# A graph transformer layer on one core: first normalisation tile by tile, query units by channel block, and a new order in the last two groups

## The reference

```python
nx = layernorm(x, ln1_g, ln1_b)
q, k, v = nx @ Wq + bq, nx @ Wk + bk, nx @ Wv + bv        # 8 heads of 64
scores = where(adj, q @ k.T / sqrt(64), -1e9)             # per graph and head
x = x + (softmax(scores) @ v) @ Wo + bo
nx = layernorm(x, ln2_g, ln2_b)
return x + gelu(nx @ W1 + b1) @ W2 + b2                   # 512 -> 2048 -> 512
```

## Time and profile before

| | |
|---|---|
| median of 3 runs | 2164.35 us (2162.98 to 2164.65) |
| profiled execution | 2164.58 us, span 2162.7 us |
| TensorE busy | 2127.7 us, 98% of the span |
| VectorE busy | 1487.9 us, 69% |
| ScalarE busy | 905.2 us, 42% |
| POOL busy | 433.7 us, 20% |
| chain that ended last | PE 96%, DVE 1%, ACT 1%, POOL 1%, DMA 1% |

### The profile page before, as it was taken

How to read it: one execution, slowest core, us unless ns; L and a number is a source line. 1 busy time by engine, 2 the same in 40 slices (tenths; PEclk the granted TensorE clock), 3 DMA queues, 4 the chain that set the end, 5 groups by cost and what they waited for, 6 DMA issues and landing times.

```text
span 2162.7 us, 33121 instructions
## 1 busy us (share of the span) xinstructions
PE 2127.7 (98%) x13216; PEld 1756.9 (81%) x13216; DVE 1487.9 (69%) x2205; ACT 905.2 (42%) x1318; POOL 433.7 (20%) x291
## 2 busy tenths in 40 slices
PE   7999999999999988999999999999999999999999
PEld 6788888888888876888888888888888888888887
DVE  4888888888999965666666656656666666656433
ACT  3444444443344443345345345345345345345332
POOL 2333433321111114003003003003003103103200
PEclk9999999999999998999999999999999999999999
DMA  4344333331222114444544544544544544544532
GB/s 147 129 153 156 135 133 133 138 124 65 70 75 70 46 50 185 156 180 172 193 180 165 199 180 165 199 174 171 199 167 173 204 160 174 209 153 174 217 126 93
DMA packets 103793, 323.98 MB, mean 150 GB/s; under 512 B 21360, under 2 KB 29552, under 8 KB 87280
## 3 DMA queue, kind: packets, MB, share of 16 engines
q1 hardware_dynamic: 98144, 321.68, 40.4%
q10 hardware_dynamic: 5520, 0.55, 0.2%
HBM read 265.57 MB, written 56.62 MB: 149 GB/s over the span
## 4 chain that ended last, share of the span: by engine, by line
PE 96%; DVE 1%; ACT 1%; POOL 1%; DMA 1%; issue 0%; SPq 0%; ACTq 0%; DVEq 0%; POOLq 0%
PE lin L181 11%; PE lin L182 10%; PE lin L183 10%; PE ps_r L181 5%; PE ps_r L182 5%; PE ps_r L183 5%; PE ps_out L181 5%; PE ps_out L182 5%; PE ps_out L183 5%; PE ps_x L181 5%; PE ps_x L182 5%; PE ps_x L183 5%; PE ps_z L181 3%; PE ps_z L182 3%; PE ps_z L183 3%; PE ps_scores L1334 2%
## 5 line engine op out<-in xcount | busy, mean ns | idle before, releaser
L1168 DVE TENSOR_TENSOR acc<-ps_r,acc 128x512 f32<-128x512 f32 x256 | 176.5, 690 | 327.8 <-PE ps_r L183 327.0
L798 ACT ACTIVATE snaps<-ps_x 128x512 f32<-128x512 f32 x192 | 114.4, 596 | 410.7 <-PE ps_x L183 410.7
L181 PE MATMUL ps_r<-w_ring,h_ring 128*128 128x512 f32 x512 | 199.6, 390 | 0.9 <-DVE h_ring L1158 0.9
L181 PE MATMUL ps_x<-nxc,w_ring 128*128 128x512 f32 x512 | 199.4, 389 | 0.0
L183 PE MATMUL ps_r<-w_ring,h_ring 128*128 128x512 f32 x512 | 199.2, 389 | 0.0
L183 PE MATMUL ps_x<-nxc,w_ring 128*128 128x512 f32 x512 | 199.2, 389 | 0.0
L182 PE MATMUL ps_x<-nxc,w_ring 128*128 128x512 f32 x512 | 199.2, 389 | 0.0
L182 PE MATMUL ps_r<-w_ring,h_ring 128*128 128x512 f32 x512 | 199.2, 389 | 0.0
L181 PE MATMUL ps_out<-w_ring,h_ring 128*128 128x512 f32 x512 | 199.2, 389 | 0.0
L183 PE MATMUL ps_out<-w_ring,h_ring 128*128 128x512 f32 x512 | 199.2, 389 | 0.0
L182 PE MATMUL ps_out<-w_ring,h_ring 128*128 128x512 f32 x512 | 199.2, 389 | 0.0
(11 more groups left out here) (131 smaller groups left out, 5131.1 us busy)
## 6 DMA issues: line engine op xcount, KB each, us to landing
w_ring<-w_scratch SPq DMA_DIRECT2D x64, 1792.0 KB, 7.3
w_ring<-w_scratch SPq DMA_DIRECT2D x64, 1024.0 KB, 7.1
xb<-x_scratch SPq DMA_DIRECT2D x22, 1024.0 KB, 10.2
xres<-in_x SPq DMA_DIRECT2D x64, 256.0 KB, 2.8
x_scratch<-xres SPq DMA_DIRECT2D x64, 256.0 KB, 2.2
x<-in_x SPq DMA_DIRECT2D x15, 1024.0 KB, 6.0
acc<-x_scratch SPq DMA_DIRECT2D x32, 256.0 KB, 2.9
out<-xb SPq DMA_DIRECT2D x32, 256.0 KB, 2.0
```

What stands on the lines that cost most here:

```text
L181: pe.matmul(out, lhs[1], rhs[0], start=first, stop=False, skip_group_check=resumed)
L798: act.activation(snaps[:, j], ps_x[:, :], ACT.Copy).then_inc(snap_done[j], 1)
L1168: dve.tensor_tensor(acc(t), ps_r[:, :], acc(t), ALU.add).then_inc(acc_added, 1)
```

## The change

**Start.** The statistics, the aggregation, the addition of epsilon, POOL's power and the norm of group 0 are done tile by tile (`first_stats`), and `var_done` and `rstd_done` count four for group 0. The transposes of group 0 go to the banks of scores and probabilities (`first_t`) instead of `lin`. `wq` comes in four transfers and is split in four pieces: ScalarE does three before the first `affine` and the fourth behind the first `nx_hi`, VectorE all four low parts. The query units are done together (`first_queries`): for each channel block c, all four units. The transposes of group 1 stand before the last three value units of group 0, and ScalarE does the four `affine` of group 1 first and then the four `nx_hi`. The statistics of group 1 come after the splits of group 0 as before.

**Last two groups.** SP issues the loads of `spare` first in every group body that has them. ScalarE does `ln_tile_affine` of tile 6 before its second `take_probT` of group 14 and that of tile 7 behind it. POOL's four sums move from group 14, where they stood before the last two biases, to group 15, behind its first `fill_neg`. In TensorE's order for group 15 F5 and P1 stand before W0.

```diff
-              ("W", 0), ("F", 5), ("P", 1), ("W", 1), ("O", 1), ("F", 6), ...
+              ("F", 5), ("P", 1), ("W", 0), ("W", 1), ("O", 1), ("F", 6), ...
...
-        return [("U", j) for j in FIRST_UNITS if g == -1] + [("T", k) for k in range(KC)]
+        units = [("U", j) for j in FIRST_UNITS]
+        return units[:-3] + [("T", k) for k in range(KC)] + units[-3:] if g == -1 else []
...
             def body(g, par):                       # SP
+                for n in ln_tiles(g):
+                    load_ln_tile(n)
                 if g + 3 < NG:
                     load_x(g + 3, 1 - par)
...
-                for n in ln_tiles(g):
-                    load_ln_tile(n)
...
-            for i, w in enumerate((wq, wk, wv)):
+            for c in range(KC):
+                sp.dma_start(raw_w[0][:, c], wq[c * P:(c + 1) * P, :]).then_inc(wq_loaded[c], 16)
+            for i, w in ((1, wk), (2, wv)):
...
-                if g == NG - 2:                     # POOL, body
-                    t_sums(0)
-                    for n in range(4):
-                        t_sum(0, n)
                 bias_xres(g, 2)
                 bias_xres(g, 3)
             def last_body(g):
                 fill_neg(g, 0)
+                t_sums(0)
+                for n in range(4):
+                    t_sum(0, n)
                 conv_lo(0)
...
-            rstd_of(0)
-            weight_lo(0, slice(KC // 2, KC))
+            for t in range(TILES):
+                pool.wait_ge(var_done, t + 1)
+                pool.tensor_tensor(rstd[:, t:t + 1], var_eps[:, t:t + 1], minus_half[:, 0:1], ALU.pow)\
+                    .then_inc(rstd_done, 1)
...
+                for n in ln_tiles(g)[:-1]:          # ACT, body
+                    ln_tile_affine(n)
                 take_probT(g, 1)
+                if g == NG - 2:
+                    ln_tile_affine(ln_tiles(g)[-1])
                 unit(9)
...
-            weight_hi(0)
+            wq_hi(0)
+            wq_hi(1)
+            wq_hi(2)
             act.wait_ge(cols_loaded, 16 * 4)
             for k in range(KC):
                 affine(0, k)
                 nx_hi(0, k)
+                if k == 0:
+                    wq_hi(3)
...
+            def first_stats(t):                     # DVE
+                ln_stats(0, 0, t)
+                dve.wait_ge(stats_done, t + 1)
+                dve.bn_aggr(moments[:, t, :], stats[:, t, :]).then_inc(moments_done, 1)
+                dve.wait_ge(moments_done, t + 1)
+                dve.tensor_scalar(var_eps[:, t:t + 1], moments[:, t, 1:2], EPS, None, ALU.add).then_inc(var_done, 1)
...
+            for t in range(TILES):
+                first_stats(t)
+                if t > 0:
+                    ln_norm(0, 0, t - 1)
+            ln_norm(0, 0, TILES - 1)
+            for c in range(3):
+                wq_lo(c)
+            for k in range(KC):
+                nx_lo(0, k)
+                if k == 0:
+                    wq_lo(3)
...
+            def first_queries():                    # PE
+                for c in range(KC):
+                    pe.wait_ge(w_lo_done[0], c + 1)
+                    pe.wait_ge(nx_split, c + 1)
+                    for m in range(KC):
+                        mm = split3(pe, lin[bank_of(-1, "U", 3 * m)][:, :],
+                                    tuple(w[0][:, c, m * P:(m + 1) * P] for w in (w_hi, w_lo)),
+                                    (nxT_hi[:, c, :], nxT_lo[:, c, :]), c == 0, c == KC - 1)
+                        if c == KC - 1:
+                            mm.then_inc(u_done, 1)
```

More of the change, by code:

```diff
@@ L298, in adj_layer @@
             ps_part = {"C11": ps_y, "C22": ps_z, "C12": ps_z}
+        first_t = [ps[:, i * HEADS // 2:(i + 1) * HEADS // 2] for ps in (ps_scores.rearrange("p h t n -> p h (t n)"), ps_probT)
+                   for i in range(2)]
+        first_t = [b.rearrange("p h n -> p (h n)") for b in first_t]
         raw_w = [qT[1][:, :, :], v[1][:, :, :], softmax.rearrange("p s (h m) t n -> p (s h) (m t n)", h=2), qT[1][:, :, :]]
@@ L310, in adj_layer @@
         w_loaded, w_hi_done, w_lo_done = ([sem(f"w{c}_{s}") for c in "qkvo"] for s in ("loaded", "hi_done", "lo_done"))
+        wq_loaded = [sem(f"wq_loaded{c}") for c in range(KC)]
         cols_loaded, rows_loaded, mlp_cols_loaded = sem("cols_loaded"), sem("rows_loaded"), sem("mlp_cols_loaded")
@@ L505, in _ @@
             load_mask(0, 0)
-            sp.wait_ge(w_lo_done[0], 2)
+            sp.wait_ge(w_lo_done[0], KC)
             sp.dma_start(raw_w[3], wo.rearrange("(c p) n -> p c n", p=P)).then_inc(w_loaded[3], 16)
@@ L531, in rstd_of @@
             def rstd_of(g):
-                pool.wait_ge(var_done, g + 1)
+                pool.wait_ge(var_done, TILES + g)
                 pool.tensor_tensor(rstd[:, :], var_eps[:, :], minus_half[:, :], ALU.pow).then_inc(rstd_done, 1)
@@ L754, in body @@
                         nx_hi(g + 2, k)
-                for n in ln_tiles(g):
-                    ln_tile_affine(n)
+                if g < NG - 2:
+                    for n in ln_tiles(g):
+                        ln_tile_affine(n)
             def job_hi(q, which):
@@ L864, in mlp_step, with wq_hi @@
                         m_affine(2 * s + (q == 6), k)
-            weight_hi(0)
+            def wq_hi(c):
+                act.wait_ge(wq_loaded[c], 16)
+                act.activation(w_hi[0][:, c, :], raw_w[0][:, c], ACT.Copy).then_inc(w_hi_done[0], 1)
+            wq_hi(0)
+            wq_hi(1)
+            wq_hi(2)
             act.wait_ge(cols_loaded, 16 * 4)
@@ L1247, in mlp_step, with wq_lo @@
                     conv_lo(s + 1, 3)
-            for g in range(2):
-                for t in range(TILES):
-                    ln_stats(g, g, t)
-                ln_var(g)
-                for t in range(TILES):
-                    ln_norm(g, g, t)
-                if g == 0:
-                    weight_lo(0, slice(0, KC // 2))
-                    for k in range(KC):
-                        nx_lo(0, k)
-                    weight_lo(2, slice(0, KC))
+            def wq_lo(c):
+                dve.wait_ge(w_hi_done[0], c + 1)
+                dve.tensor_tensor(w_lo[0][:, c, :], raw_w[0][:, c], w_hi[0][:, c, :].bitcast(F32),
+                                  ALU.subtract).then_inc(w_lo_done[0], 1)
+            for t in range(TILES):
[5 more added lines that the diff above has]
+                wq_lo(c)
+            for k in range(KC):
+                nx_lo(0, k)
+                if k == 0:
+                    wq_lo(3)
+            weight_lo(2, slice(0, KC))
+            for t in range(TILES):
+                ln_stats(1, 1, t)
+            ln_var(1)
+            for t in range(TILES):
+                ln_norm(1, 1, t)
             weight_lo(3, slice(0, KC))
@@ L1305, in unit @@
                 if is_first(g) and m == 0:
-                    pe.wait_ge(w_lo_done[which], 2 if which == 0 else 1)
+                    pe.wait_ge(w_lo_done[which], 1)
                 for c in range(KC):
@@ L1385, in body @@
                     elif kind == "U":
-                        unit(g + 1, n, take_bank(g, "U", n))
+                        if is_first(g + 1) and n % 3 == 0:
+                            if n == 0:
+                                first_queries()
+                        else:
+                            unit(g + 1, n, take_bank(g, "U", n))
                     elif kind == "O":
```

10 lines of the change are left out of this document (5 added, 5 removed).

## The result

The changed kernel takes 2148.5 us (median of 6 runs, 2148.22 to 2150.96), the kernel before in the same comparison 2163.35 us (median of 6, 2161.71 to 2164.65). The ratio is 0.9934 with a 95% interval of 0.9922 to 0.9947: faster, by 14.3 us by the ratio and 14.9 by the medians. The forecast was 13.0 us and 2151.4 us. The profiled execution took 2148.46 us with a span of 2146.4, so the two profiles lie 16.3 us apart in span, since the one of before stood above its median.

What follows compares the result with a forecast made beforehand. TensorE's own work bounds the steady groups; idle time lies before 60 us and from 770 to 842 us. 3.3 + 1.3 + 5.4 + 3.0 = 13.0 us off 2164.35 gives 2151.4 us, range 2146.5 to 2157.5.

Steps and rivals of the forecast that it cites:

- Part 1: Start, group 0 tile by tile: first product 3.3 us earlier, moved transposes of group 1 1.3 us more; 4.6 us.
- Part 2: Group 14, spare loads first: prob wait goes, but a new 2.9 us attT_lo wait before W0; 0.3 to 1.9 us left.
- Part 3: Group 15, POOL's sums after biases and memset: O0 5.4 us earlier, after a new wait of about 4.0 us.
- Part 4: Group 15, F5 and P1 before W0: 4.5 us loss at W0 goes, new slow stretch at O0 costs 1.7; 3.0 us.
- No meetings: Rival, groups 14 and 15: POOL and VectorE pass each other, norm 6 is not held; 2147.8 us, 20%.
- Pieces land together: Rival, start and end: wq pieces land at once, and more POOL and VectorE meetings; 2155 to 2156.4 us, 16%.
- the end gives nothing: Rival, last groups: stores, tile and xres loads collide, only the start is left; 2159.8 us or within 0.2%, 6%.
- The slower case: Rival, group 15: POOL's sums 1 and 2 hold conv_hi and the softmax, some 20 us late; 2168.7 us, 3%.

Runs made afterwards that it cites:

- experiment 10: Changed kernel with wq loaded in one transfer, all four pieces waiting for it: 2149.22 us, ratio 0.9937.
- Experiment 3: Kernel before with only SP's tile loads moved first in its group bodies: 2162.75 us, ratio 0.9997.
- experiment 1: Changed kernel with its last two groups as before, so only the start is new: 2158.92 us, ratio 0.9979.
- experiment 8: Changed kernel with POOL's low splits in group 15 held back until prob of unit 0 is done: 2153.57 us, ratio 0.9958.
- Experiment 5: Changed kernel with POOL's a_rstd of tile 6 ahead of the two biases of group 14: 2147.4 us, repeated 2146.87 us.
- experiment 4: Changed kernel with W0 back in front of F5 and P1 in group 15: 2152.87 us, ratio 0.995.
- experiment 2: Kernel before with only the edits of groups 14 and 15, start as before: 2152.72 us, ratio 0.9951.
- experiment 6: Changed kernel with a_rstd of tile 6 before group 14's biases and group 15's second memset before the low splits: 2145.8 us, repeated 2147.07 us.
- experiment 7: Changed kernel with only the second memset of group 15 moved ahead of the first low split: 2151.55 us, ratio 0.9949.

## Why the prediction was right, and where its sizes were off

**Part 1, the start: right.** The first product was forecast 3.3 us earlier and came 3.2 us earlier. Between it and the first scores of group 0 another 1.1 us came that was not in the sum: the low level lasted 3.5 us where I had taken the 5.7 of before. It is near the lower of the two bounds that I gave (3.2 to 8 us; no profile shows 8). This 1.1 us is luck of the profiled execution as much as a gain: nine profiles have the changed kernel's start; in eight of them the low level of these products lasted from 2.7 to 5.7 us, in the ninth there was none. In the nine the first scores of group 0 start between 48.28 and 50.95, in the three profiles with the start of before between 53.73 and 54.47. The moved transposes gave 1.05 us instead of 1.3, since the second query unit of group 1 still waits 0.8 us for its low half. From 4.6 forecast to 5.1 in the profile, and 4.5 to 4.8 us when timed alone. The pieces from one queue landed one after another (experiment 10). The Trainium skill (DMA: Bandwidth & Descriptors, section Two DMAs through the same engine are not ordered) warns that a later transfer may complete before an earlier one; no run here shows that.

**Part 2, loads first: right in the mechanism, the wait too small.** The wait for `prob` went, and a wait for `attT_lo` took its place, because `a_rstd` stood behind two biases and a memset. I had 2.9 us with a slow stretch as possible, and it was 3.84 us with a slow stretch (granted 0.57, some 1.6 us). The step that was off is the moment of the biases. In before's clock the norm came at 774.8 (769.71 + 5.1) and not at 773.4, because the pair of biases began at 769.9 and not at 768.3; its length beside `prob` was nearly as worked out (3.50 us, forecast 3.7). The `xres` loads now stand behind the `spare` loads on SP. I had left them where they were. Experiment 3 shows the same pair at 769.67 and the norm at 774.31. A second slow stretch of the same kind followed the 2.49 us wait at W2, where in the profile of before a wait of the same length had none. It is not shown to be of the change's making: experiments 1 and 3 have before's order of TensorE, POOL and ScalarE there, and in their profiles the same wait is followed by it (granted 0.53 and 0.55). So by the scores of group 15 TensorE was only 2.4 us earlier than before, 2.7 us less than the start had given, 1.6 of them by that second stretch; I had expected 0.3 to 1.9 us more.

**Part 3, POOL's queue: the term right, for a partly different reason.** O of group 15 came 5.4 us earlier than the start alone would make it, as forecast, because V, the softmax chain and POOL set that moment and not TensorE. In before's clock the second memset ended at 822.1 (816.96 + 5.1), forecast 822.25. Inside it two sizes cancel: the sums began 1.2 us later than I had them (800.55 + 5.1 = 805.65 against 804.45, since the last `xres` load hangs on VectorE's residuals, which stand behind the late norm of tile 6: they started at 789.53 + 5.1 = 794.6, before at 794.53, and I had them 1.2 us early), and the meetings cost POOL 1.0 us (5.76 for 4.74) and not 2.4. That the two cancel to 0.2 us is luck. The larger loss was on VectorE's side, where `prob` took 3.04 us for 1.23 and ended at 817.16, level with the memset, so both bind. That contention is real (experiment 8), as the Trainium skill has it (SBUF — State Buffer, section Who interferes with whom). That the term would be 7.8 us without it stays worked out, not measured. What differs is how TensorE passed the time. I had it wait 4.0 us and run slow behind it; it came late by the two slow stretches of group 14, and waited only 0.7 us. Experiment 5 shows the same account from the other side: without the early losses the wait of 4.0 us is there, with its slow stretch.

**Part 4 and after: right in sign, 1.9 us too small.** The 3.0 us had 1.7 us for a slow stretch behind O of group 15. There is none (granted 1.00 from 821.80 to 826.00), which makes it 4.7 of the 4.9 us measured. Taken by itself the new order is worth 3.5 to 4.4 us (experiment 4) against my 4.5.

**Outside the sum:** 0.9 us in the MLP, where the wait for `h_ring` is 0.2 us and was 0.9 before. I had no term for it. The way from the last residual to the end takes 1302.5 to 1305.3 us in the fourteen profiles, whose code is the same from there on, so 0.9 us is no more than executions differ by, and no run took it apart.

**Rivals.** "No meetings" would have given 2147.8 us, nearer to the measured median than my own figure, but its mechanism did not happen: the biases of group 14 and a subtraction, `prob` and both splits of group 15 each met an operation of the other engine. The time came near it by the shorter low level at the start, the missing slow stretch at O and the 0.9 us in the MLP. "Pieces land together" is refuted by the first pieces of `wq_hi` at 8.58 us and by experiment 10, "the end gives nothing" by experiment 2. The slower case needed POOL's chain some 20 us late; its second sum ended 1.2 us later than forecast.

**Open.** Why a wait of 2.5 us at W2 of group 14 is followed by the low level in one execution and not in another of the same kernel is not settled (both profiles of experiment 5, and both of experiment 6, differ in it). It may be a large part of the spread of the runs; that wasn't tested. And no kernel here keeps POOL and VectorE apart without holding POOL back, so what meetings cost in all was not measured. Of the start only the order of the query units and the four transfers were run by themselves: what the norm tile by tile, the other banks and the earlier transposes each give is read from the profile, not from a run.

## What to carry to other kernels

When a load is pulled forward, follow the consumer to its next input before counting the gain: here the loads first gave nothing alone, since the next step hung on another engine's queue. When work is moved beside another engine's operations with two operands from SBUF, count a meeting as the other's whole remaining duration and look at what each edit moves next to what: a memset pulled forward had to wait for ScalarE, held POOL's splits back and so placed a subtraction behind one of them, and the kernel was 3 us slower. And a wait of TensorE that is removed early can come back later in the same chain, so account at the point that sets the end, not at the wait.

## What the runs showed of the hardware

**Meetings are all or nothing, and the one that began first is served first.** In the changed kernel POOL's last sum ends at 810.36 and the subtraction on VectorE, begun at 809.77, at 811.45, 1.1 us behind it; in experiment 7 the sum ends at 810.69 and the subtraction at 811.78, again 1.1 us behind, though it had begun 2.2 us before that end. So a subtraction of 1.22 us took 1.68 in the one and 3.30 us in the other. POOL's side stretches likewise: 3.50 us for two biases of 2.5, 5.76 us for two splits of 4.74. So these two engines do not meet at semaphores alone.

**The norm is held as well.** In experiment 5 the normalisation of a tile (one tensor and two columns, 0.55 us elsewhere) took 1.50 us beside the biases:

```profile
765.35 1.50 DVE L1101 TENSOR_SCALAR spare<-spare,a_moments,a_rstd 128x512 f32<-128x512 f32 x1
```

**The low level follows short waits, but not always.** It followed waits of 2.16 us (experiment 4), 3.84 and 2.49 us (changed kernel) and 3.96 us (experiment 5, first profile). It did not follow waits of 2.49 us at W2 before the change, of 2.50 us there in the first profiles of experiments 5 and 6, nor one of 2.58 us at W0 in experiment 7. In experiments 5 and 6 the second profile of the same kernel has the slow stretch behind the same wait of 2.49 us: from there to the scores of group 15 7.2 and 7.0 us pass instead of 5.65. Each slow stretch costs about 1.6 us. At the start the granted clock reads 1.00 while products are 0.43 us apart; there only their spacing tells the level. How long it lasts there differs between executions of the same instructions: counted from the first product, 3.5 us in the changed kernel, 4.4 in experiment 4, 5.7 in experiment 7, 2.7 in experiment 8, and in the repeat of experiment 6 the products come 0.23 us apart from the second on. Between the shortest and the longest lie 2.7 us at the first scores of group 0 (48.28 and 50.95), more than most of the differences between kernels here.

**A transfer pulled ahead pushes the one behind it.** The `xres` pair landed 3.9 us after its issue behind the `spare` loads (issued at 760.83, biases from 764.76), where before, ahead of them, it took 2.7 us (765.60 and 768.26).
